# Two transformer layers on one core: products in halves, nine banks rectified by VectorE, the first shift in the exponential's bias, and new step tables

## The reference, cut to what matters

```python
xn = layernorm(x)
x = x + differential_attention(xn) + linear_with_fp6_blocks(xn)   # layer 0
xn = layernorm(x)
x = x + rotary_attention(xn) + sign_mlp(xn)                       # layer 1
```

## Time and profile before

| | |
|---|---|
| median of 3 runs | 824.66 us (824.35 to 825.26) |
| the profiled execution | 823.92 us |
| its span, first to last instruction | 822.0 us |
| mean granted TensorE clock | 0.996 |
| ScalarE, TensorE, VectorE, GpSimd busy | 93%, 91%, 67%, 8% |

### The profile page before, as it was taken

The page is one execution under the profiler, slowest core; times in us unless marked ns, Lnnn a source line. Parts: engine busy times, 40 slices in busy tenths (PEclk is TensorE's granted clock), DMA queues, the critical chain, the costliest instruction groups (busy, mean ns, idle before and its releaser), DMA issues.

```text
span 822.0 us, 17919 instructions
## 1 busy us (share of the span) xinstructions
PE 749.1 (91%) x6751; PEld 244.5 (30%) x6751; DVE 550.6 (67%) x1186; ACT 760.8 (93%) x856; POOL 64.0 (8%) x84
## 2 busy tenths in 40 slices
...
GB/s 105 182 41 178 76 95 177 95 2 77 143 74 134 14 78 142 115 93 22 109 137 140 33 53 133 94 162 9 96 129 88 119 2 106 102 1 79 142 14 14
DMA packets 45933, 73.99 MB, mean 90 GB/s; under 512 B 7344, under 2 KB 23344, under 8 KB 45712
## 3 DMA queue, kind: packets, MB, share of 16 engines
...
q10 hardware_dynamic: 64, 0.10, 0.0%
...
## 4 chain that ended last, share of the span: by engine, by line
PE 56%; ACT 22%; DVE 11%; issue 8%; DMA 1%; SPq 1%; DVEq 0%; POOL 0%; ACTq 0%
PE ps_pv L1004 23%; ACT probs L823 21%; PE ps_s L985 13%; PE ps_misc L848 7%; PE ps_misc L844 7%; PE ps_misc L849 5%; PE ps_misc L837 2%; DVE pv_sb L1535 1%; ACT ff_out L775 1%; SPq L510 0%; DVE stat L1078 0%; DMA thirds_dram<-qk_thirds 0%; DMA k_ab<-thirds_dram 0%; DVE xn L1116 0%; DVE qk_thirds L1289 0%
## 5 line engine op out<-in xcount | busy, mean ns | idle before, releaser
L823 ACT ACTIVATE probs<-ps_s 128x1024 f32<-128x1024 f32 x768 | 724.5, 1055 | 29.2 <-PE ps_s L985 28.3
L1004 PE MATMUL ps_pv<-probs,v_aug 128*32 128x512 f32 x3072 | 409.8, 605 | 9.0 <-ACT probs L823 4.5
L985 PE MATMUL ps_s<-q_ab,k_ab 32*128 32x512 bf16 x896 | 88.6, 385 | 27.9 <-ACT probs L823 24.6
L985 PE MATMUL ps_s<-q_c,k_c 32*128 32x512 f32 (+1 forms) x640 | 80.9, 494 | 21.5 <-ACT probs L823 20.1
L1004 PEld LDWEIGHTS ps_pv<-probs,v_aug 128*32 128x32 f32 x3072 | 61.3, 108 | 100.5 <-issue 76.7
L848 PE MATMUL ps_misc<-h_hi,k_w 128*128 128x512 f32 x192 | 87.8, 457 | 0.4 <-DVE tmp L1299 0.3
L1239 DVE CAST h_hi<-ff_out 128x512 fp32r<-128x512 f32 x64 | 27.3, 427 | 89.2 <-ACT ff_out L775 85.7
L849 PE MATMUL ps_misc<-h_lo,k_w 128*128 128x512 f32 x192 | 75.8, 395 | 0.0
L985 PEld LDWEIGHTS ps_s<-q_ab,k_ab 32*128 32x128 bf16 x896 | 22.7, 91 | 165.0 <-ACT probs L823 136.3
L1535 DVE STREAM_TRANSPOSE pv_sb<-ps_pv 128x512 f32<-128x512 f32 x48 | 34.4, 717 | 54.0 <-PE ps_pv L1004 52.0
L985 PEld LDWEIGHTS ps_s<-q_c,k_c 32*128 32x128 f32 (+1 forms) x640 | 30.7, 181 | 120.6 <-ACT probs L823 99.1
...
## 6 DMA issues: line engine op xcount, KB each, us to landing
...
```

Of the source, the lines that this page charges most:

```text
L823: nc.scalar.activation(probs[:, U.slot(s), 2 * half:2 * half + 2], ps_s[:, 2 * pair:2 * pair + 2], ACT.Exp, bias=0.0 if U.first else -SCAL ...
L985: ins = nc.tensor.matmul(ps_s[:, bank, :], k[row:row + n, slot, c * P:(c + 1) * P], q[row:row + n, slot, :], start=True, stop=True)
L1004: ins = nc.tensor.matmul(ps_pv[32 * j:32 * j + 32, :], v_aug[:, U.v, c, a:a + 32], probs[:, U.slot(s), j, :], start=c == 0 and not odd, st ...
```

## The change

- **Halves.** Nine new item names (`q0_a`, `k0_a` and so on) make a job's product for tokens 0 to 255, and the item without `_a` makes the rest. The taker takes the whole bank after the second. The first half waits for the bank as the whole job did. For q and k the matmuls have 256 columns instead of 512 and are twice as many.
- **Nine banks by VectorE** (`DIRECT`): ScalarE no longer copies these; VectorE makes the high part as max(ps_misc, 0) and the low part as max(ps_misc, 0) minus the high part, both from PSUM, and releases the bank after the second.
- **The first shift in the bias.** The exponential of the first two units has the bias of the others. The shift rows hold zeros, which SP loads early; for the heads of `fast` slots 0 and 1 the zeros come with the `fast` results. In the branch for large weights, not taken here, VectorE adds the exact shift. SP issues eight transfers for it instead of four.
- **The start.** `fast` runs in the order q 0, k 0, q 1, k 1; step 0 waits for k 0, step 1 for q 1. `WARM_AGAIN` is gone.
- **New tables.** Most items keep their step, some move by one to three.

The core of the diff (of the tables: a piece of the first, the loop body, a piece of the last):

```diff
-WARM_AGAIN = 16
-PE_ONLY = ("ff1", "ff2")
+HALVES = ("q0_a", "k0_a", "v0_a", "q1_a", "k1_a", "v1_a", "quant_mm_a", "project0_a", "project1_a")
+PE_ONLY = ("ff1", "ff2", *HALVES)
+DIRECT = (("ff0", 1, 0), ("ff0", 2, 0), ("ff0", 3, 0), ("ff0", 4, 0), ("ff0", 5, 0), ("ff0", 6, 1), ("ff1_b", 6, 3), ("ff1_b", 7, 1), ("ff1_b", 7, 3))
...
-            ("fast", 0, "q", 0), ("fast", 0, "q", 1), ("fast", 0, "k", 0), ("q0", 0), ("k0", 0), ("exact0", 0)]
+            ("fast", 0, "q", 0), ("fast", 0, "k", 0), ("fast", 0, "q", 1), ("q0", 0), ("k0", 0), ("exact0", 0)]
...
+    {0: [("norm0", 1, 4), ("regroup", 0, "A", 0)], 1: [("take", 0, "A", 1), ("x_t0", 1), ("regroup", 0, "A", 1), ("bias", 0)],
+     2: [("q0_a", 1), ("q0", 1)], 3: [("quant", 1, 0), ("lambda", 0)], 4: [("quant", 1, 1), ("quant", 1, 2), ("k0_a", 1)],
+     6: [("k0", 1), ("quant", 1, 3), ("quant", 1, 4)], 7: [("exact0", 1), ("v0_a", 1), ("take", 0, "B", 0)], 8: [("v0", 1),
+     ("quant", 1, 5)], 9: [("quant", 1, 6), ("bias", 1)], 11: [("regroup", 0, "B", 0)], 12: [("quant_mm_a", 1),
...
 LOOP = [
+    {0: [("ff0", -1, 0), ("take", -2, "C", 1)], 1: [("ff0", -1, 1)], 2: [("q1_a", -1), ("regroup", -2, "C", 1), ("q1", -1)],
+     4: [("k1_a", -1), ("rope", -1, "q", 0), ("out_t1", -2), ("rope", -1, "q", 1)], 5: [("k1", -1)], 7: [("rope", -1, "k", 0),
+     ("rope", -1, "k", 1), ("ff0", -1, 2)], 8: [("v1_a", -1), ("take", 0, "A", 0), ("v1", -1)], 9: [("regroup", 0, "A", 0)],
+     10: [("qk_norm1", -1)], 11: [("ff0", -1, 3)], 12: [("project1_a", -2), ("project1", -2), ("norm0", 1, 0),
+     ("norm0", 1, 1)], 13: [("ff1", -1, 0, 0), ("ff1", -1, 0, 1), ("ff1", -1, 0, 2), ("ff1_b", -1, 0), ("norm0", 1, 2)],
+     14: [("exact1", -1), ("norm0", 1, 3), ("ff1", -1, 1, 0)], 15: [("ff1", -1, 1, 1), ("ff1", -1, 1, 2), ("ff1_b", -1, 1)]},
+    {0: [("ff1", -1, 2, 0), ("ff1", -1, 2, 1), ("take", 0, "A", 1)], 1: [("ff1", -1, 2, 2), ("norm0", 1, 4),
+     ("ff1_b", -1, 2)], 2: [("x_t0", 1)], 3: [("regroup", 0, "A", 1)], 4: [("quant", 1, 0), ("q0_a", 1), ("q0", 1)],
+     5: [("quant", 1, 1)], 6: [("ff1", -1, 3, 0), ("ff1", -1, 3, 1), ("quant", 1, 2)], 7: [("quant", 1, 3), ("quant", 1, 4),
+     ("ff1", -1, 3, 2), ("ff1_b", -1, 3)], 8: [("k0_a", 1)], 9: [("take", 0, "B", 0), ("k0", 1)], 10: [("quant", 1, 5),
+     ("quant", 1, 6)], 12: [("bias", 1)], 13: [("quant_mm_a", 1), ("quant_mm", 1)], 14: [("exact0", 1)], 15: [("ff2", -1, 0),
+     ("regroup", 0, "B", 0), ("take", 0, "B", 1), ("regroup", 0, "B", 1)]},
+    {1: [("combine", 0, 0), ("ff2", -1, 1)], 2: [("combine", 0, 1), ("combine", 0, 2)], 3: [("ff2", -1, 2), ("ff2_b", -1)],
+     4: [("combine", 0, 3), ("v0_a", 1)], 5: [("v0", 1)], 6: [("combine", 0, 4)], 7: [("ff_t", -1), ("combine", 0, 5),
+     ("out_t0", 0)], 9: [("take", -1, "C", 0), ("project0_a", 0), ("project0", 0)], 10: [("norm1", 0, 0)],
+     12: [("norm1", 0, 1), ("norm1", 0, 2)], 13: [("norm1", 0, 3), ("norm1", 0, 4)], 14: [("x_t1", 0)],
+     15: [("regroup", -1, "C", 0)]},
...
+     13: [("ff1_b", 6, 1)], 14: [("ff1", 6, 2, 0),
+     ("regroup", 7, "B", 0), ("ff1", 6, 2, 1)], 15: [("ff1", 6, 2, 2), ("ff1_b", 6, 2), ("ff1", 6, 3, 0), ("ff1", 6, 3, 1),
+     ("ff1", 6, 3, 2), ("ff1_b", 6, 3)]},
...
+def tiles_of(item):
+    name, *args = item
+    if name in HALVES:
+        return range(T // 2)
+    return range(T // 2 if (name + "_a", *args) in PLAN.before else 0, T)
...
-                                             bias=0.0 if U.first else -SCALE[U.layer] * BOUND[U.layer], scale=SCALE[U.layer]).then_inc(exps_made, 1)
+                                             bias=-SCALE[U.layer] * BOUND[U.layer], scale=SCALE[U.layer]).then_inc(exps_made, 1)
...
-                    ins = in_columns(ps, w, xn_t[:])
+                    ins = in_columns(ps[:, tokens], w, xn_t[:, tokens])
...
                         if s == 0:
-                            warm(WARM_AGAIN)
                             wait_taken(pe, ("fast", 0, "k", 0))
-                            pe.wait_ge(shift_loaded["A0"], SHIFTED)
+                        elif s == 1:
+                            wait_taken(pe, ("fast", 0, "q", 1))
...
+                if (name, b, f) in DIRECT:
+                    dve.wait_ge(job_made, PLAN.made[name, b, f])
+                    settled()
+                    nc.vector.tensor_scalar(hi, ps_misc[:], 0.0, None, ALU.max).then_inc(ff_split, 1)
+                    dve.wait_ge(ff_split, n + 1)
+                    nc.vector.scalar_tensor_tensor(lo, ps_misc[:], 0.0, hi.bitcast(F32), ALU.max, ALU.subtract).then_inc(ff_split, 1)
+                    dve.wait_ge(ff_split, n + 2)
+                    dve.sem_inc(job_taken, 1)
```

More of the change, by code:

```diff
@@ L71 @@
              qk_norm1="dve", w_t="dve", quant_mm="dve",
-             project0="dve", project1="dve", ff0="act", ff1="act", ff1_b="act", ff2="act", ff2_b="act", ff_t="dve",
+             project0="dve", project1="dve", ff0="act", ff1_b="act", ff2_b="act", ff_t="dve",
              fast="dve")
-PE_ONLY = ("ff1", "ff2")
+HALVES = ("q0_a", "k0_a", "v0_a", "q1_a", "k1_a", "v1_a", "quant_mm_a", "project0_a", "project1_a")
+PE_ONLY = ("ff1", "ff2", *HALVES)
+DIRECT = (("ff0", 1, 0), ("ff0", 2, 0), ("ff0", 3, 0), ("ff0", 4, 0), ("ff0", 5, 0), ("ff0", 6, 1), ("ff1_b", 6, 3), ("ff1_b", 7, 1), ("ff1_b", 7, 3))
@@ L95 @@
-    {1: [("x_t0", 2)], 2: [("combine", 0, 1)], 3: [("combine", 0, 2), ("q0", 2), ("combine", 0, 3), ("combine", 0, 4),
[8 rows of a table removed]
-     14: [("quant", 2, 3), ("quant", 2, 4), ("ff1", 0, 1, 2)]},
-    {0: [("quant", 2, 5), ("quant", 2, 6), ("ff1_b", 0, 1)], 1: [("ff1", 0, 2, 0), ("ff1", 0, 2, 1), ("take", 1, "B", 1),
-     ("ff1", 0, 2, 2)], 2: [("ff1_b", 0, 2)], 3: [("regroup", 1, "B", 1), ("bias", 2), ("combine", 1, 0), ("combine", 1, 1),
-     ("quant_mm", 2)], 4: [("combine", 1, 2)], 5: [("combine", 1, 3)], 6: [("combine", 1, 4), ("combine", 1, 5),
[4 rows of a table removed]
+    {0: [("v0_a", 0), ("v0", 0)], 1: [("fast", 0, "k", 1)], 2: [("setup", 0)], 5: [("quant", 0, 0), ("quant", 0, 1)],
+     6: [("quant", 0, 2), ("quant", 0, 3), ("quant", 0, 4)], 8: [("take", 0, "A", 0)], 10: [("quant", 0, 5), ("quant", 0, 6)],
+     12: [("quant_w", 0), ("norm0", 1, 0)], 13: [("w_t", 0), ("norm0", 1, 1), ("norm0", 1, 2)], 14: [("quant_mm_a", 0),
+     ("quant_mm", 0)], 15: [("norm0", 1, 3)]},
```

131 lines of the change are left out of this document (80 added, 51 removed), and 97 rows, old and new, of tables (FIRST, LAST, LOOP).

## The result

The kernel after takes 815.3 us (median of 4 runs, 814.21 to 815.76) against 824.5 us for the kernel before (4 runs, 823.88 to 825.26): ratio 0.9884, 95% interval 0.9871 to 0.9897. The profiled execution took 815.69 us, its span is 813.9. The forecast was 816. The sum behind it, 8.8 us, is to be held against the profiled executions, 823.92 - 815.69 = 8.2 us.

What follows compares the result with a forecast made beforehand. ScalarE (93% busy) and TensorE (91%) were taken to share the limit. Terms for start, pinned starts, loop and single units summed to 8.8 us off 823.92: 815.1, median about 816, range 813 to 819.

Steps and rivals of the forecast that it cites:

- The start, +1.5 at unit (B, 1): New start and the chain behind it, through VectorE and the projection in (A, 1): unit (B, 1) starts 1.5 us earlier.
- rival (b): Half clock again after TensorE idles at (A, 1), before v0 and at (A, 7): about 1.2 us each, 818.5; chance 0.10.
- The pins: Starts of (A, 1), (A, 7), (C, 7) wait for the load of k: (A, 1) 0.35 us earlier, (A, 7) 1.1, (C, 7) nothing through.
- rival (a): Pins don't hold: 1.7 us at (A, 1), 1.3 more at (A, 7), 0.5 at (C, 7) come through, 812.5; chance 0.12.
- The loop, 3.2: Four loop bodies gain 0.31 us from a direct bank and 0.48 from halves each, 3.2 us in all.
- The halves' 0.48 a body: Split jobs in the loop: k1 0.15, k0 0.13, v0 with the respread ff2 products 0.2 us per body.
- The direct bank's 0.31: ff0 bank taken directly by VectorE at the head of units (A, 2) to (A, 6): 0.31 us per place.
- (C, 0) 0.76 for 1.0: Unit (C, 0): quant_mm, v0, the projection and ff2 apart gain about 1.0 us.
- (C, 5) got nothing of 0.35: Unit (C, 5): ff2 over three steps gains 0.35 us.
- the last bank's 0.15: Last of the three ff1_b direct banks: 0.15 us gained.
- Rival (d): Slower: first halves wait for the shared bank at 21 places; at 0.7 us each, 830; chance 0.05.
- Rival (c): Part of the gains doesn't arrive: direct form costs the next ff0, crowded steps lose more; 819 to 823; chance 0.07.

Runs made afterwards that it cites:

- the first execution: First profiled execution of the kernel after, unchanged: 815.69 us.
- the second execution: The kernel after, unchanged, run and profiled once more: 815.78 us in the median, profiled execution 815.43 us.
- the fifth experiment: The kernel after with no halves, each split job whole in the step of its second half: 820.28 us, ratio 0.994.
- the fourth: The kernel after with an empty list of direct banks, ScalarE copying all 64 again: 819.08 us, ratio 0.9928.
- tenth: The kernel after with unit (B, 7)'s products spread and k0 (7) moved to steps 4 and 5 of unit (B, 6): 813.63 us, ratio 0.9869.
- the eighth experiment: The kernel after with five more direct banks, ff0 (b, 3) for b from 1 to 5: 817.97 us, ratio 0.9924.
- the seventh: The kernel after with the last ff1 products of unit (B, 7) spread to earlier steps: 813.47 us, ratio 0.9865.

## Why the prediction came out as it did

The time was right, and the mechanism of the start and of the loop. That 8.8 us forecast meets 8.2 and 8.5 measured is in part luck: in the first execution the start gave 1.84 less than its term, and (C, 5), (C, 0), (C, 7) and (B, 1) together 0.97 less; the loop gave 1.20 more, (B, 6) 0.45, (B, 7) 0.29 and (A, 6) 0.17 more.

**The start, +1.5 at unit (B, 1).** The chain was right: scores at 20.34, (B, 0) 0.50 earlier (forecast 0.55), projection at 98.83 (98.9; for the earlier trace rows), unit (B, 1) 1.48 earlier, all in the second execution. In the first the half clock of rival (b) took 2.0 us of it, and the term was -0.34. I had priced such a stretch at 1.2, from one of 3.4 us; this one lasted 6.8. Whether the clock falls varies between executions: it fell behind v0 in 4 of the 8 profiled executions with that idle stretch and in none of the 4 with warm transposes in it. (The page "TensorE: Matmul & The Clock Gate" of the Trainium skill, section "What's actually happening", says that the number of slow matmuls at a kernel's start varies from run to run of the same kernel. The traces agree that it varies, and not for the first matmuls alone: `fast k 1` takes 1.94 us in one execution of the kernel after and 1.06 in the other, which has its fall at 640.) Rival (b) and the forecast were not two cases but two executions of one kernel.

**The pins.** At (A, 1) the step that failed is the pin itself. I read it from the row of the weights; the scores and ScalarE in the kernel before are

```profile
81.84 0.40 PE L985 MATMUL ps_s<-q_ab,k_ab 32*128 32x512 bf16 x4 [0.42 <-ACT probs L823]
...
78.84 5.61 ACT L823 ACTIVATE probs<-ps_s 128x1024 f32<-128x1024 f32 x6 [0.20 <-PE ps_s L985]
```

The scores waited for an exponential, as in any step, and ScalarE ran through the start without a gap: the load had landed at 81.37. So "18.96 us" holds 0.4 us that is no transfer, and the forecast "TensorE idles about 2 us" met 0.50 and 0.42. In the second execution the cast came at 63.14 (forecast 62.5), the load 17.3 us later, and the unit starts 0.90 earlier, released by ScalarE; the steps themselves allowed 0.90 and not 2. This is rival (a)'s mechanism, though for 0.55 us only, since the projection holds what follows. The way from cast to scores isn't a constant either: where the scores wait for the load it takes 17.9 to 19.1 us at (A, 1) and 17.4 to 18.8 at (A, 7). At (A, 7) cast to scores is 17.4, 18.5 and, before, 18.2: of the 1.55 us gained in (B, 6) 0.73 is the earlier cast (forecast 1.1) and 0.83 the load; in the second execution the load took back 0.31. Unit (A, 7) gained 1.16 with a full clock (forecast 1.4) and 0.65 with half clock (forecast 0.9): its step 15 takes 2.08 where it took 1.81. (C, 7) is pinned as forecast: steps 8 to 14 of (C, 6) are 0.88 shorter and step 15, with the wait, 0.79 longer. No run takes the new places in (B, 6) and (A, 7) away by themselves, nor the new start; their gains are read from the traces.

**The loop, 3.2.** The mechanism was right, the size 4.4. The halves' 0.48 a body is the fifth experiment's 0.48, though not in the shares given (k1 0.08, k0 0.08, v0 0.32 instead of 0.15, 0.13, 0.2). The direct bank's 0.31 is 0.54 in the fourth: from the unit's start to step 3's scores it is 5.83 us, against 6.40 before and my 6.08; I had allowed for late events that don't come (the PV at 3.97, not 4.13). The remaining 1.18 - 0.48 - 0.54 = 0.16 is left to the new places of other jobs; it wasn't tested by itself.

**The rest.** (C, 0) 0.76 for 1.0, though the halves alone are worth 1.0 there: a new place costs 0.24, which I did not follow. (B, 7)'s step 15 takes 5.36 (forecast 5.2); it costs 0.16 and not 0.45, as other steps of the unit gained. (C, 5) got nothing of 0.35: ff2's spread gives 0.27, as the fourth and tenth experiments have it (32.35), and in the kernel after step 10 takes 2.19 instead of 1.83. There the PV waits 0.78 us for VectorE's transpose, ahead of which VectorE idles 0.46. The tenth has the same direct banks and not this idle; where it comes from is open. (B, 1)'s 0.1 and the last bank's 0.15 didn't come. Rival (d) fell, since without halves the kernel is slower, but the wait it counted at (A, 1) is there: step 4, with the first half of k0, takes 2.78 us, and 1.82 without halves. Rival (c) fell for this kernel and is true of the eighth experiment's.

Why the seventh's kernel is better by 1.8 in the median where its unit gives 1.0 is not settled: its profiled execution had no fall of the clock before the end, its load for (A, 7) took 17.5 us against 17.4 and 18.5, and the intervals of the two ratios (0.9851 to 0.988, 0.9871 to 0.9897) overlap.
